# Earlier first loads in attention 0, inputs loaded into x1 and biased ahead, and pair 1's splits moved to the end of the middle stage

## The reference, cut to what matters

```python
x = layernorm(x + attn0(x))   # 16 heads of 8, causal, decay -|i-j|, softmax
x = layernorm(x + moe(x))     # 8 experts, top-1 routing, 128 -> 512 -> 128
x = layernorm(x + attn1(x))   # 16 heads of 64, rmsnorm of q and k, gated causal bias, softmax
x = layernorm(x + ffn1(x))    # 128 -> 512 -> 512 -> 512 -> 128
```

## Time and profile before

| | |
|---|---|
| median of 3 runs | 2282.85 us (2277.38 to 2283.62) |
| the profiled execution's own time | 2285.02 us |
| its span (first to last instruction) | 2283.2 us |
| TensorE busy | 2072.3 us (91%) |
| VectorE busy | 1513.8 us (66%) |
| ScalarE busy | 1210.0 us (53%) |
| GpSimd busy | 779.2 us (34%) |
| mean granted TensorE clock | 0.951 of full |

### The profile page before, as it was taken

How to read it: one execution, slowest core, us unless ns; L and a number is a source line. 1 busy time by engine, 2 the same in 40 slices (tenths; PEclk the granted TensorE clock), 3 DMA queues, 4 the chain that set the end, 5 groups by cost and what they waited for, 6 DMA issues and landing times.

```text
span 2283.2 us, 34398 instructions
## 1 busy us (share of the span) xinstructions
PE 2072.3 (91%) x11728; PEld 1169.3 (51%) x11728; DVE 1513.8 (66%) x3409; ACT 1210.0 (53%) x1923; POOL 779.2 (34%) x480
## 2 busy tenths in 40 slices
PE   5899999998487999877999999999999999999998
PEld 2333333334476555544555555555555555655644
DVE  3877777774732778865888878888887875333311
ACT  2366666667343678853656555555565553223232
POOL 5000000000601111003777777777777773000000
PEclk7899999999588999986999999999999999999999
DMA  5233333111265579656666666666666667543300
GB/s 177 95 125 128 120 120 127 57 51 62 98 186 145 172 231 293 200 169 141 170 166 170 165 152 152 150 159 169 163 169 152 164 158 209 135 103 84 88 5 9
DMA packets 230189, 319.11 MB, mean 140 GB/s; under 512 B 22316, under 2 KB 152668, under 8 KB 229608
## 3 DMA queue, kind: packets, MB, share of 16 engines
q1 hardware_dynamic: 214712, 289.04, 46.2%
q0 software_dynamic: 7664, 24.39, 3.0%
q10 hardware_dynamic: 7640, 3.48, 0.5%
HBM read 176.91 MB, written 105.84 MB: 124 GB/s over the span
## 4 chain that ended last, share of the span: by engine, by line
PE 28%; DVE 16%; issue 8%; SPq 1%; DMA 1%; ACT 0%; DVEq 0%
PE ps L1252 10%; DVE a1mx L968 4%; PE ps L916 4%; DVE a1KB L982 3%; DVE a1mx L972 3%; PE ps L900 3%; DVE a1QB L982 3%; PE ps L870 2%; PE ps L901 2%; PE ps L1203 2%; DVE a1mx L965 2%; PE ps L1263 1%; PE ps L1240 1%; PE ps L1241 1%; DVE ps L965 1%
## 5 line engine op out<-in xcount | busy, mean ns | idle before, releaser
L1088 POOL TENSOR_TENSOR a1sum<-a1sum,a1prob 128x1024 f32<-128x1024 f32 (+3 forms) x256 | 489.0, 1910 | 64.9 <-ACT a1prob L1025 33.5
L1025 ACT ACTIVATE a1prob<-ps 128x512 f32<-128x512 f32 (+2 forms) x640 | 326.0, 562 | 252.7 <-PE ps L903 238.4
L468 DVE TENSOR_REDUCE a0grid<-ps 128x8 f32<-128x1024 f32 x288 | 346.7, 1221 | 118.9 <-PE ps L344 64.9
L569 ACT ACTIVATE a0prob<-ps 128x1024 f32<-128x1024 f32 x288 | 292.9, 1025 | 170.2 <-PE ps L370 91.3
L965 DVE CUSTOM_DVE_ANT_0 ps<-ps,c_mask_ij 128x128 f32<-128x128 f32 x496 | 262.7, 551 | 97.2 <-issue 95.5
L900 PE MATMUL ps<-a1QA,a1KA 69*128 69x512 f32 (+3 forms) x768 | 285.7, 379 | 5.8 <-PEq L33 3.4
L916 PE MATMUL ps<-a1prob,a1V 128*64 128x512 f32 (+3 forms) x1536 | 277.9, 505 | 0.0
L870 PE MATMUL ps<-a1KA,a1QA 68*128 68x128 f32 x744 | 241.7, 391 | 28.7 <-DVE a1mx L968 16.4
L901 PE MATMUL ps<-a1QB,a1KB 128*128 128x512 f32 (+3 forms) x768 | 264.4, 352 | 0.0
L916 PEld LDWEIGHTS ps<-a1prob,a1V 128*64 128x64 f32 x1536 | 104.4, 140 | 171.1 <-issue 144.2
L1085 POOL TENSOR_TENSOR a1sum<-a1prob 128x768 f32<-128x768 f32 x64 | 156.8, 2450 | 82.0 <-ACT a1prob L1025 79.9
(11 more groups left out here) (268 smaller groups left out, 3227.5 us busy)
## 6 DMA issues: line engine op xcount, KB each, us to landing
a1FK<-s_k SPq DMA_DIRECT2D x128, 256.0 KB, 5.3
a1FQ<-s_q SPq DMA_DIRECT2D x128, 256.0 KB, 5.8
s_xs<-c_zero POOLq DMA_DIRECT2D x19, 1024.0 KB, 9.0
s_q<-mqkT SPq DMA_DIRECT2D x32, 512.0 KB, 3.0
s_k<-mqkT SPq DMA_DIRECT2D x32, 512.0 KB, 3.0
s_v<-mv SPq DMA_DIRECT2D x32, 512.0 KB, 3.9
a1V<-s_v SPq DMA_DIRECT2D x32, 512.0 KB, 4.4
a1KA<-a1KB SPq DMA_DIRECT2D x64, 256.0 KB
```

What stands on the lines that cost most here:

```text
L468: dve.tensor_reduce(grid[g % 2][:, :, a:b + 1:b - a], banks(("max", k)), axis=AX.X, op=ALU.max).then_inc(s1_free, 1)
L569: act.activation(prob[:, :, a:b + 1:b - a, :], banks(("exp", q)), ACT.Exp).then_inc(p_full, 1)
L1025: act.activation(weights_of(g, u)[:, group[0]:group[-1] + 1, off:BANK], both(e, u, group), ACT.Exp).then_inc(weighed, 1)
L1088: pool.tensor_tensor(t[:, :, off:BANK], t[:, :, off:BANK], weights_of(g, u)[:, :, off:BANK], ALU.add).then_inc(summed, 1)
```

## The change

1. attention0: three places for high and low (`PARTS3`), with three `stored` semaphores. `EARLY` is 13 and no longer 17. ScalarE issues its load of BK after product 7 and no longer after product 15. SP loads K and BQ of group 0 after the store of chunk 2 and no longer before it, and Q and BK of group 1 after the store of chunk 4 and no longer of chunk 3. The wait for the stores stands at the head of a load (`batch_stored`).
2. middle, start: the whole input is loaded in two halves into `x1`, the place in which the norm leaves its result, which now lies past attention0's tiles. GpSimd adds the bias to all 8 chunks ahead of the barrier. The scatters follow each other without a bias between them.
3. middle, end: the first 12 maxima of pair 0, then the last gates, then the other 12. ScalarE then makes pair 1's four splits, into tiles QB1 and KB1 that exist from the start, and issues the row of pair 0's maxima.
4. attend_and_finish, pair 0: SP issues the four copies before `load_e(1)`. VectorE's `lower(1, ...)` stand at units 0 to 3 and no longer 2 to 5. ScalarE's splits of pair 2 stand after units 0, 3, 4 and 5 and no longer after 4 to 7.

```diff
-    EARLY, NPROD, COL = 17, len(products), dim + 1
+    PARTS3, EARLY, NPROD, COL = 3, 13, len(products), dim + 1
...
-        high, low = ([over(f"{n}{r}", [P, 2, CHUNK], F32R) for r in range(2)] for n in ("high", "low"))
+        high, low = ([over(f"{n}{r}", [P, 2, CHUNK], F32R) for r in range(PARTS3)] for n in ("high", "low"))
...
+        def batch_stored(engine, b):
+
+            for c in range(b * seq // CHUNK, (b + 1) * seq // CHUNK):
+                engine.wait_ge(stored[c % PARTS3], 16 * 4 * (c // PARTS3 + 1))
...
             store(1)
+            batch_stored(sp, 0)
             still(sp, Q[0], "q0", 0, loaded1[0])
-            sp.wait_ge(cleared, 1)
-            load_second(sp, 0)
             for c in range(2, chunks):
                 store(c)
-                if c == 3:
+                if c == 2:
+                    sp.wait_ge(cleared, 1)
+                    load_second(sp, 0)
+                if c == 4:
                     sp.wait_ge(cleared, 2)
                     load_first(sp, 1)
...
-                if c > 1:
-                    act.wait_ge(stored[c % 2], 16 * 4 * (c // 2))
+                if c >= PARTS3:
+                    act.wait_ge(stored[c % PARTS3], 16 * 4 * (c // PARTS3))
...
             cast_constants()
-            for n in range(6, EARLY - 1):
+            for n in range(6, 8):
                 drain(n)
             act.wait_ge(cleared_first, 1)
+            batch_stored(act, 0)
             moving(act, BK[0], "k0", 0, loaded1[0])
-            for n in range(EARLY - 1, NPROD):
+            for n in range(8, NPROD):
                 drain(n)
```

```diff
-            load_e(1)
             for k in range(SPLIT):
                 copy_high(1, k)
+            load_e(1)
             for k in range(PARTS):
                 load_f(2, k)
...
-                    if g == 0 and 2 <= u < 6:
-                        lower(1, u - 2)
+                    if g == 0 and u < 4:
+                        lower(1, u)
...
                     exponentials(g, u)
-                    if g == 0 and u < 2:
-                        split(1, 2 * u)
-                        split(1, 2 * u + 1)
-                    at_units = (0, 3, 4, 5) if g > 0 else (4, 5, 6, 7)
-                    if g + 2 < G and u in at_units:
-                        split(g + 2, at_units.index(u))
+                    if g + 2 < G and u in (0, 3, 4, 5):
+                        split(g + 2, (0, 3, 4, 5).index(u))
```

```diff
-        def load(c):
-
-            if c > 1:
-                nc.sync.wait_ge(joined, c - 1)
-            nc.sync.dma_start(x[c % 2][:, :, :], ins["x"][chunk(c), :].rearrange("(t p) d -> p t d", p=P)).then_inc(x_in[c % 2], 16)
+        def load(half):
+
+            t = slice(half * NTILE // 2, (half + 1) * NTILE // 2)
+            nc.sync.dma_start(x1[:, t, :], ins["x"][t.start * P:t.stop * P, :].rearrange("(t p) d -> p t d", p=P)).then_inc(x_in[half], 16)
...
-        def gpsimd_ahead():
-
-            nc.gpsimd.wait_ge(w_first, 16 * len(first))
-            bias(0)
-            bias(1)
+            pool.wait_ge(w_first, 16 * len(first))
+            for c in range(steps):
+                pool.wait_ge(x_in[c // (steps // 2)], 16)
+                to = x1[:, c * TILES:(c + 1) * TILES, :]
+                pool.tensor_tensor(to, to, bo[:, :].unsqueeze(1).to_broadcast([P, TILES, P]), ALU.add).then_inc(biased, 1)
...
-            if n == LAST:
-                here += [("max", k, 0) for k in range(NM)] + [("turn", 0, 0)]
+            here += [("max", k, 0) for k in range(NM // 2)] if n == LAST else []
             here += [("aug", c, 0) for c in turn_gates.get(n, ())]
+            here += [("max", k, 0) for k in range(NM // 2, NM)] + [("turn", 0, 0)] if n == LAST else []
...
+            act.wait_ge(pair0.loaded_f[1], 16 * 8)
+            for k in range(4):
+                which, head = k % 2, k // 2
+                buf, wide = ((pair0.FK[1], pair0.KB1), (pair0.FQ[1], pair0.QB1))[which]
+                act.activation(wide[:, head, :], buf[:, head, :], ACT.Copy).then_inc(pair0.rounded, 1)
+            act.wait_ge(pair0.max_done, NM + 1)
+            act.dma_start(pair0.QA[ROW:ROW + 1, :, :].bitcast(F32), pair0.neg[:, 0, :].bitcast(F32)).then_inc(pair0.row_in, 16)
```

More of the change, by code:

```diff
@@ L173, in part @@
             b, m = divmod(g, per)
-            if h == 0:
-                for r in range(2):
-                    engine.wait_ge(stored[r], 16 * 4 * (b + 1))
             row, to = (m * H + h) * dim, base_of(h // PAIR) + FIRST + 3 * (h % PAIR) * dim
@@ L420, in tensor_program @@
                 project(n)
-            for n in range(8, EARLY - 3):
-                drained(n)
+            for n in range(8, EARLY - 1):
+                if n % 8 < 2 * RING:
+                    drained(n)
             pe.wait_ge(const["c_cast"], 4)
@@ L1472, in middle @@
         own("gap", [P, max(0, const["a0_end"] - nc.sbuf_base) // 4 + 8])
-        tri_f, x = own("trif", [P, P]), [own(f"xin{r}", [P, TILES, P]) for r in range(2)]
+        tri_f, x1 = own("trif", [P, P]), own("x1", [P, NTILE, P])
         wo, bo, cent = own("wo", [P, P]), own("bo", [P, P]), own("cent", [P, experts])
@@ L1517, in sync_first @@
                 nc.sync.dma_start(d, s).then_inc(w_small, 16)
-            load(2)
             for d, s in rest:
                 nc.sync.dma_start(d, s).then_inc(w_rest, 16)
-            for c in range(3, steps):
-                load(c)
             nc.sync.wait_ge(made, 5)
```

71 lines of the change are left out of this document (35 added, 36 removed).

## The result

| | before | changed |
|---|---|---|
| median, 20 runs each on one chip | 2281.76 us (2276.62 to 2287.88, and one run of 5275.1) | 2275.95 us (2272.36 to 2281.3) |
| the profiled execution's own time | 2285.02 us | 2273.5 us |
| its span | 2283.2 us | 2271.7 us |
| mean granted TensorE clock | 0.951 | 0.955 |

The ratio is 0.9977, with a 95% interval of 0.9969 to 0.9985: a gain of 5.2 us (5.8 by the two medians), where 15.4 were forecast. Two repeats on other chips gave 0.998 (0.997 to 0.999) and 0.9996 (0.9987 to 1.0005). The two profiled spans differ by 11.5 us, because the two executions lie near opposite ends of their kernels' runs; 4.1 us of it fall behind pair 0, where both programs do the same. So the pieces are compared with repeated profiles further down.

The account below looks back on a forecast made before the run. TensorE is busy for 91% of the span, so gains come only where it, or what it waits for, stands still. Lead-in -10.4, scatters -7.0 and pair 0 +2 make -15.4 from 2282.85: 2267.5 us, range 2258 to 2276.

Parts of the forecast that it names:

- the lead-in: Start of the first attention: earlier load of BK and shorter loop together, -10.4 us.
- so nothing queued there is late: Lead-in loop, SP's queue: moved loads and stores delay nothing, as store 3's place is wanted only by chunk 6.
- pair 0: Last attention: ScalarE's wait for pair 2's FK and FQ costs +4, later savings -2; sum +2 us (-3 to +6).
- the scatters: Middle stage: no late input, no biases between, so scatters end at 620.5 instead of 627.57: -7.0 us (-4.8 to -8.5).
- the middle's end: Gates between the two halves of pair 0's maxima: row leaves later, scores begin at 1032.3; 0 us (-1 to +1).
- Load of BK: Lead-in: BK of group 0, issued earlier, lands at 34.0 instead of 41.06, a gain of 7.1 us (2.9 to 12).
- at the 71 GB/s of the earlier trace this takes 10.9 us: Lead-in: time for the 0.77 MB of Q and BK of group 0, issued from 21.6, so ending at 33.7.
- The sentence on the Trainium skill's rule: Lead-in: 16-row parts would use only two DMA engines, taking some 12 us, with BK landing at 35.
- The loop: Lead-in, first maxima to first scores: four more units with products cost 3.0, stalls vanish; net -3.3 us (0 to -6).
- transfers stay slow: Rival, lead-in: BK lands at 38, Q and BK of group 1 late at unit 18; lead-in -5, 2273 us; chance 0.14.
- Biases ahead: Before the middle stage: input loads and GpSimd's 8 biases, 10.2 us, near attention0's end cost nothing.
- 3.7 MB take 16.3 us: Pair 0: transfers up to pair 2's FK and FQ, at 227 GB/s, last from 1033 to about 1050.

Follow-up runs that it names:

- store2_late: Changed kernel, but SP issues store 2, K and BQ only once Q and BK of group 0 have landed: 1.0002 of the kernel before.
- kbq_late: Changed kernel, but SP issues K and BQ of group 1 after the row of group 0's maxima: 1.0013 of the kernel before.
- kbq_last: Changed kernel with K and BQ of group 1 behind group 0's row and Q and BK of group 2: 0.9947 of the kernel before, 2269.24 us.
- last_split: Changed kernel with the load order of kbq_last and pair 2's splits after units 4 to 7, old layout: 0.9915 of the kernel before.
- layout: Changed kernel with scratch tensors s_q and s_k ordered head, high or low, dimension, token: 0.9933 of the kernel before, 2265.84 us.
- bias_between: Changed kernel with biases of chunks 2 to 7 back after the barrier, at their old places, input still loaded ahead: 1.0005 of the kernel before.
- end_undone: Changed kernel with the middle stage's old end: all 24 maxima, the row, then the last gates: 0.9994 of the kernel before.
- split_late: Changed kernel with pair 2's splits after units 4 to 7 again in pair 0: 0.9962 of the kernel before, 2275.34 us.
- after_third: Changed kernel without any edit, repeated on another chip: 0.9996 of the kernel before.

## Why the prediction failed, step by step

Two terms made the miss. In the lead-in the step "so nothing queued there is late" failed, since the row took 9.0 us instead of 2.6 to arrive, and Q and BK landed 2.9 us after their forecast. In pair 0 the wait had the right cause and the wrong size (+6.8 instead of +2). In numbers, -4.4 instead of -15.4: the lead-in gave 8.2 us less, pair 0 cost 4.8 us more, and the scatters and the middle's end gave 1.0 us more each.

**Load of BK** (forecast 34.0, measured 36.6 to 37.5 in all profiles with this lead-in; before, 40.4 to 42.2. The gain is 4.4 us, not 7.1). The issue moved as said. The step that failed is "at the 71 GB/s of the earlier trace rows this takes 10.9 us": an average over a stretch with parts of both sizes, whereas the last parts run at 45 GB/s with a share of two engines. (The 96 rows of 4 KB, twice, are 0.79 MB and not 0.77, which adds 0.2 us, and the first bytes moved some 0.8 us after the issue, not 1.2.) Its other premise, that K and BQ no longer travel beside Q and BK, didn't hold either: SP issues store 2 at 28.48 and K right behind it.
```profile
30.34 4.64 SPq L184 DMA_DIRECT2D a0K<-s_k  x8
```
But store2_late, where they wait, has BK only 0.7 us earlier, so that this cost little. The sentence on the Trainium skill's rule gave 35, and I kept it beside the sum; it was nearer.

**The loop** (forecast 45.5 us from first maxima to first scores; 44.0 to 46.3 where the row is not held up: kbq_late, kbq_last, last_split and the kernels with the layout). The stalls for a place are gone and the units count as worked out. The term was right in size, -3.3 against some -4, but it was not realised, because of the next point.

**"So nothing queued there is late"** was the step that cost most. I had followed the queue as far as chunk 6's place and not to the row that ends the lead-in. The loop is shorter, so the row is due at 78.4 and no longer at 87.3; and K and BQ of group 1 with two stores then stand right before it. They take 9.0 us to clear, not 2.6. So the profiles show 50.3 to 53.1 us for this loop, against 48.9 to 49.9 before. The lead-in gave 2.2 us instead of 10.4, less than the least of its bounds (2.9). With the row's way clear, in kbq_last, the stage starts at 549.0, 6.8 us earlier than the mean of the changed kernel. The rival "transfers stay slow" had the cause (backlog) but the wrong victim: Q and BK of group 1 at unit 18 were in time.

**Biases ahead** (0): right, GpSimd had them done at 545.9, 8 us before the stage.

**Scatters** (-7.0, measured -8.0 without halts): right in mechanism and nearly in size. The sum took 3.5 us for the input's wait; bias_between confirms that half by what it keeps (3.7), and the rest by what it loses (3.9).

**Middle's end** (0, 1 either way): the scores follow the row's issue by 2.0 us, as forecast. From the experts' first load to the scores it is 1.0 us less, at the bound; by end_undone's median the new order is worth about 3 us together with what it does to pair 0. That is at most a small error: neither the 1.0 us nor the 3 is clear of the noise.

**Pair 0** (+2, up to +6; measured +6.8). The mechanism was right: ScalarE idle behind its first exponential, arrow to FQ. The sizes were off: "3.7 MB take 16.3 us" and the first kept result 22 us after the first scores. Measured were 21.05 us to the first split, in which 202 GB/s moved 4.3 MB at full share, and 25.8 us. More was moved up to then than I counted, and at a lower rate. The first maxima of pair 1 came 8.8 us after the first scores, not the 5.7 of the forecast's "about 38". What was to go later, -2, came to -1.0 (32.5 us from the first kept result to pair 0's end, 33.5 before). So pair 0 lies just past the bound of +6, and the lead-in just past its own bound on the same, slow side. split_late shows the same pair 0 at 48.7 without that wait: the change had a gain of 3 us there, and one loop condition turned it into a loss of 7. Which of the other moves (pair 1's splits ahead, the copies first, the lowerings earlier) gives the 3 us, no run separates.

**The range and the rivals.** 2276 was the upper end and 2275.95 came out. That it lies inside by 0.05 us is luck: the same chip's kernel before had a median of 2281.76 in the end, 1.1 us under the 2282.85 from which I subtracted, and on another chip the changed kernel gave 2282.72. The outcome, less than 0.3% faster, had a chance of 0.06. Of the rivals, "transfers stay slow" (2273) came nearest, and it needed pair 0's upper bound as well. I let the terms' bounds add up as if chance would balance them, while two of them rested on one resource, the transfers.

## What to carry to other kernels

When a chain is shortened, list again what stands in each queue ahead of its last small transfer: it will be issued earlier, into a backlog that had drained before. Look at the busy share of the DMA engines while something waits for a load: 0.1 to 0.2 of 16 is the share of two or three engines, which here was a matter of the access pattern and was mended in the tensor's layout. And don't put an operation that waits for a bulk load right behind the first instruction of a pipeline; here, four activations moved up by two to four units cost 9.6 us, more than all of the lead-in's gain.

## What the runs showed of the hardware

**Two engines.** A part of 16 rows of 4 KB whose source is two blocks of 8 rows travels with the share of about two engines at 45 to 53 GB/s; with 16 evenly spaced rows there, Q and BK took half the time. SP's issue also got shorter, here for the 8 parts of BQ, in the changed kernel and in layout:
```profile
35.03 4.31 SPq L184 DMA_DIRECT2D a0BQ<-s_q  x8
```
```profile
32.46 2.76 SPq L184 DMA_DIRECT2D a0BQ<-s_q  x8
```
The layout also changes where the stores write; what that does by itself, no run shows.

**VectorE's halts.** On two of the five chips used for the experiments, VectorE stood still two to four times for 1.5 to 5.5 us in the middle stage: in all eight profiles there at the last choice, in seven at the last locate, in five at the join of chunk 5 or 7. In the other profiles, with the same instructions, never. In the pieces above they take 4 of the scatters' 8 us, which fits a gain of 0.2% without them and of nothing with them. One thought is the fetching of the program: the Trainium skill (Runtime: NRT & Kernel Launch, Instruction fetch mechanics) says that it comes in blocks of 256 instructions by a queue of its own, mostly hidden. The trace of after_third speaks against it: its last two halts are 3.4 us and some five instructions apart, and during all three of its halts the DMA view shows nothing but the scatters' queue. It does show transfers of instructions elsewhere, the nearest between 590 and 600 us and behind 616. No run here settles what the cause is, nor whether the kernel before has them too and hides them behind GpSimd's longer row of work.
